# Routing six of the eight groups inside the second attention, in place of five

## The reference, cut to what matters

```python
x = x + _L0_xattn_ref(_layernorm(x), ctx_2048, ...)
x = x + _L0_ffn_ref(_layernorm(x), ...)
x = x + _L1_xattn_ref(_layernorm(x), ctx_2048, ...)   # ends in a layer norm of its own
x = x + _L1_ffn_ref(_layernorm(x), ...)
```

```python
shared = jnp.maximum(normed @ sw1 + sb1, 0.0) @ sw2 + sb2
scores, idx = jax.lax.top_k(probs, TOPK)              # TOPK = 2 of E = 8
w = scores / (jnp.sum(scores, axis=-1, keepdims=True) + 1e-06)
```

## Time and profile before

| | us |
|---|---|
| median of 3 runs | 1467.87 (1464.55 to 1470.46) |
| the profiled execution, its own time | 1472.39 |
| span in that profile | 1470.6 |
| `attention1`, its last instruction ends | 1161.86 |
| `sorted_experts`, its first instruction starts | 1163.17 |
| its first expert matmul starts | 1195.53 |

### The profile page before, as it was taken

How to read it: one execution, slowest core, us unless ns; L and a number is a source line. 1 busy time by engine, 2 the same in 40 slices (tenths; PEclk the granted TensorE clock), 3 DMA queues, 4 the chain that set the end, 5 groups by cost and what they waited for, 6 DMA issues and landing times. The chain is left out here.

```text
span 1470.6 us, 35946 instructions
## 1 busy us (share of the span) xinstructions
PE 1252.5 (85%) x13401; PEld 1044.1 (71%) x13401; DVE 1053.2 (72%) x2080; ACT 898.4 (61%) x1699; POOL 652.2 (44%) x677
## 2 busy tenths in 40 slices
PE   4999998399999999997699999999996268999780
PEld 3777776278777877785589888888885256788660
DVE  5888888566777687775356678989887477687563
ACT  3888887566565656554455655666654258788560
POOL 3222222145555565564332345556664435066461
PEclk9999999699999999999799999999999559999995
DMA  4222221332212221321300000000000122147536
GB/s 142 93 93 93 94 93 64 116 94 80 73 48 82 80 73 43 87 80 48 100 26 10 10 16 10 17 20 17 20 14 16 50 74 84 31 152 252 178 125 183
DMA packets 88373, 109.64 MB, mean 75 GB/s; under 512 B 13322, under 2 KB 55050, under 8 KB 88202
## 3 DMA queue, kind: packets, MB, share of 16 engines
q1 hardware_dynamic: 83210, 97.05, 21.1%
q0 software_dynamic: 4992, 10.30, 2.1%
HBM read 61.70 MB, written 29.82 MB: 62 GB/s over the span
## 5 line engine op out<-in xcount | busy, mean ns | idle before, releaser
L830 POOL TENSOR_TENSOR b_h_lo<-b_h,b_h_hi 128x512 fp32r<-128x512 f32 x168 | 216.5, 1294 | 179.3 <-ACT b_h_hi L854 178.9
L849 ACT ACTIVATE b_zg<-b_zg 128x512 f32<-128x512 f32 x168 | 97.6, 581 | 82.0 <-PE b_zg L894 81.8
L854 ACT ACTIVATE b_h_hi<-b_h 128x512 fp32r<-128x512 f32 x168 | 105.1, 626 | 65.4 <-DVE b_h L1059 65.3
L2173 POOL DMA_INDIRECT planes_dram<-d_y_out,d_back x92 | 94.0, 1022 | 106.7 <-DVE d_y_out L2484 83.6
L1059 DVE TENSOR_TENSOR b_h<-b_zg,b_uw 128x512 f32<-128x512 f32 x168 | 116.1, 691 | 32.0 <-ACT b_zg L849 26.7
L1052 DVE TENSOR_TENSOR b_uw<-b_zu,b_gw 128x512 f32<-128x512 f32 x128 | 88.1, 688 | 57.7 <-PE b_zu L894 50.9
L2453 DVE TENSOR_TENSOR d_h_lo<-d_h,d_h_hi 128x512 fp32r<-128x512 f32 x124 | 85.1, 690 | 48.4 <-ACT d_h_hi L2214 37.2
L312 POOL TENSOR_TENSOR a_qx<-a_qT,headmask 128x256 f32<-128x256 f32 x64 | 37.9, 613 | 149.3 <-ACT a_qT L347 149.3
L519 DVE TENSOR_REDUCE a_top<-a_score_ps 128x8 f32<-128x1024 f32 x64 | 78.0, 1218 | 18.6 <-PE a_score_ps L410 18.6
L1293 POOL TENSOR_TENSOR c_prob<-c_prob,c_recip 128x512 f32<-128x512 f32 x64 | 65.5, 1044 | 50.9 <-DVE c_recip L1709 50.9
L1716 DVE TENSOR_TENSOR c_oT_lo<-c_oy,c_oT_hi 128x512 fp32r<-128x512 f32 x64 | 43.7, 683 | 58.3 <-ACT c_oT_hi L1421 57.8
(11 more groups left out here) (393 smaller groups left out, 4175.2 us busy)
## 6 DMA issues: line engine op xcount, KB each, us to landing
rows_dram<-a_blank SPq DMA_DIRECT2D x32, 520.0 KB, 3.3
b_gw<-gates_dram SPq DMA_DIRECT2D x64, 256.0 KB, 3.8
d_up_slot<-d_up_tab SPq DMA_DIRECT2D x15, 512.0 KB
d_down_slot<-d_down_tab SPq DMA_DIRECT2D x15, 512.0 KB
d_xg<-rows_dram SPq DMA_DIRECT2D x23, 260.0 KB
b_gm<-gates_dram SPq DMA_DIRECT2D x32, 160.0 KB, 3.9
c_craw<-in_c_ctxT_dram SPq DMA_DIRECT2D x16, 256.0 KB, 3.0
d_pay<-planes_dram SPq DMA_DIRECT2D x12, 256.0 KB, 4.2
```

The lines of the kernel that those rows point to most:

```text
L830: pool.tensor_tensor(h_lo[:, m % HS, :], h[:, m % HF, :], h_hi[:, m % HS, :].bitcast(F32), ALU.subtract).then_inc(lo_done.sem, 1)
L849: act.activation(zg_ps[:, n % ZG, :], zg_ps[:, n % ZG, :], ACT.Silu).then_inc(sg_done.sem, 1)
L854: act.activation(h_hi[:, m % HS, :], h[:, m % HF, :], ACT.Copy).then_inc(hi_done.sem, 1)
L2173: pool.indirect_dma_start(planes, bass.IndirectOffsetOnAxis(ap=back[:, t, u:u + 1], axis=0), y_out[:, t % 2, u, :], None).then_inc(added[t ...
```

## The change

One constant. Group 5 (the sixth) is now routed in `attention1`, at ticks 30 to 38, and its eight scatters take the place of group 4's at the head of `sorted_experts`; group 4's eight scatters move into ticks 35, 36 and 37. `sorted_experts` routes two groups (6 and 7) in place of three.

```diff
@@ -36,7 +36,7 @@
 UNITS = B * N // P
 GROUP = 4
 GROUPS = UNITS // GROUP
-ROUTED = 5
+ROUTED = 6
 COLS = GROUP * P
 H = 16
 PAIRS = H // 2
```

## The result

The changed kernel takes **1483.01 us** (median of 5 runs, 1477.84 to 1486.4), the kernel before on the same chip 1468.63 (1464.55 to 1472.79). The ratio is **1.0075, 95% interval 1.0046 to 1.0103**: slower, by 0.75%. Forecast were 1475.7 us and +7.8 us; the medians differ by 14.4, and 1483.01 stands at the upper end of the range that was given (1468 to 1483).

A forecast was written before the change was run, and what follows sets the result against it. PE bounds the attention's middle, but in its drain no engine does, only a chain of short steps. Drain loss 13.9 less last-stage gain 6.1 gives +7.8 us; 1467.87 + 7.8 = 1475.7 us, range 1468 to 1483.

The forecast's parts named there:

- T: Time the attention's drain loses by routing group 5 there: 13.9 us, its last instruction ending at 1175.8 instead of 1161.9.
- The six scatters: POOL's queue behind the last compare: six scatters of group 4 take 7.4 us ahead of unit 31's output scaling.
- the two last ones: Group 4's last two scatters, on POOL behind unit 31's output scaling: 0.15 + 2.4 us, landing 1.40 later.
- DVE's own detour is hidden: Drain's end: DVE's choose(5), 2.05 us ahead of the normalisation, is hidden under POOL's scatters.
- The shift up to tick 34: Drain: group 5's added steps shift the chain by 0.8 + 0.35 = 1.2 us (rounded), lower bound 0.
- The drain's end: End of the attention, what the drain loses without the earlier shift: 12.7 us.
- The fill, 3.2 us behind the landing: Drain's end: group 5's fill waits for the last scatters' landing, takes 3.2 us and ends the attention at 1175.8.
- Table loads hidden: Drain, ACT: two more function set switches for group 5, 1.28 us per load, hidden under other work.
- S: Time the last stage gives back with one group less to route: 2.9 + 3.15 = 6.1 us, bounds 2.9 and 10.2.
- Gives back all of it: Rival, last stage: PE's clock stays high and POOL's pieces are no limit, S = 13.2, total 1468.6 us; chance 0.2.
- The drain hides the routing: Rival, drain: half-idle engines hide the routing, T only 1.2 us, total 1463.0 us; chance 0.07.
- One more stall: Rival, drain: a second unexplained ACT wait adds 3.5 us, total 1479.2, or 1482.4 with S at its lower bound; chance 0.15.

The follow-up runs named there:

- e1: The changed kernel with three of group 4's scatters put ahead of group 5's compare in POOL's queue; ratio to before 1.011.
- e2: The changed kernel with all eight of group 4's scatters behind the last output scaling; ratio to before 1.0208.
- f1: The changed kernel with group 4's payload in its own memory, its eight scatters at the last stage's head, DVE splitting all weight pieces; 1442.27 us, ratio 0.9966.
- e6: The changed kernel without group 5's router products (POOL multiplies 8 values in place of 1024, routing by stale products); 1476.77 us, ratio to before 1.0116.
- e3: The kernel before with DVE splitting all of the last stage's weight pieces, POOL none; ratio to before 1.0012.
- e4: The changed kernel with DVE splitting all of the last stage's weight pieces, POOL none; ratio to before 1.005.
- e5: The changed kernel with a second payload tile, so group 5's fill and place don't wait for group 4's scatters; ratio to before 1.011.
- f3: The changed kernel with only the first unit's two copies of group 5's fill made, the other six left out; ratio to before 1.0104.
- f2: The changed kernel with group 4's payload in its own memory and its eight scatters at the last stage's head, weight splits unchanged; 1453.27 us, ratio 1.0029.
- r0: The changed kernel run again, unedited, beside others on one chip; 1477.53 us, ratio to before 1.0121.

## Why the prediction was right and where not

The sign and the mechanism held, the size did not: +7.8 was forecast, the medians differ by 14.4. That the result still falls in the range is in part luck of direction: T was priced too low, and had it been as much too high, the change would hardly have been told from none.

- **The six scatters (7.4), the two last ones (2.55), landing 1.40**: measured 7.51 from the first's start to the scaling, 2.79, 1.40. Right, and e1, e2 and f1 show that they are the cause: without them the stage starts 9.1 us earlier. That "DVE's own detour is hidden" was right too, and is also why only 4.1 of the 7.5 come back in e2: the 4.15 left are DVE's.
- **The shift up to tick 34, "1.2 us, rounded": the mis-sized term. It measured 5.4.** 3.8 arises by subtract(31): 0.8 for the variance steps as forecast, 3.0 for DVE standing still behind group 5's products (e6). I priced the products on POOL's timeline alone. The row to read was in the profile of before: there two instructions took long, each under a product of an earlier group, and 0.19 and 0.17 where none ran:
```profile
1062.15 1.45 DVE L1803 TENSOR_TENSOR c_raw<-c_raw,c_r_rstd 128x32 f32<-128x32 f32 x1
1073.93 2.22 DVE L1682 TENSOR_SCALAR c_top<-c_top 128x16 f32<-128x16 f32 x1
```
In the middle, with PE the bound, this was hidden; in the drain it is paid. The other 1.6 of the 5.4 I can't pin on one step, since after has two "remote" waits ahead of the output copy and before has one. e3 and e4 are the fairer pair: they have before's and after's attention, ran on one chip, and each has one such wait in the drain, of 2.77 and 2.76. There the output copy stands 28.41 and 29.45 behind subtract(31), so the term measures 3.8 + 1.0 = 4.9. The 1.0 is fill(4), whose slack the forecast held to cover the delay ("If it were gone, up to 1.2 us would be paid"): in e4 fill(4) waits 4.41 us for group 3's last scatter and the copy follows it without a gap, and in e5, where fill(4) waits for none of group 3's, the copy stands at 28.22. (In after 0.70 us lie between the two, so there the fill does not hold the copy.)
- **The drain's end**, from the output copy to the stage's start: 22.66 in after and 10.12 in before, 12.5 us more, where the forecast had 12.7.
- **The fill, 3.2 us behind the landing**: right in sum, wrong in mechanism. Stage start behind last scatter's end was forecast as 1.4 + 3.2 + 1.3 (the gap of before), 5.9; it is 5.07. But with the fill shortened or moved it stays (f3, e5).
- **Table loads hidden**: right, with no drain behind them.
- **S = 6.1**: 6.7 in after, and by the mechanism named. e4, and f1 against f2, show the limit that I named, POOL's pieces.
- **The rivals.** "Gives back all of it" did not come true, but an S near its 13.2 did in e4 (13.0), with another edit, and there the clock rose too: 43 to 53 us behind the stage's start PE had 0.66 of its clock in before, 0.83 in after and 1.00 in e4. "The drain hides the routing" fell with the 18.0. "One more stall": a second "remote" wait did appear in after, but most of T's excess is the products' (3.0): e3 and e4, with one such wait each, still give T = 68.20 - 50.79 = 17.4.
- **What the profiles don't explain.** Their stages sum to +10.6 us and the medians differ by 14.4, because before's profiled execution (1472.39) was 3.8 us above its median and after's was its median. But r0 and f3 differ from their before by 15.6 and 14.6 as well, and f3 has no "remote" wait. T would be larger without such waits: f3 takes 67.76 from subtract(30) to the stage's start, and before without one would take about 48.2 (e3's 50.79 less the 2.6 by which the copy comes later in e5, with one wait, than in f1, with none). This estimate gives T = 19.6, and with S = 6.9 (98.29 - 91.37) +12.7; the last 2 us of f3's 14.6 stay open.

## What to carry to other kernels

In a drain, where each engine waits for the next, price an added instruction not only in its own queue but for every engine that runs beside it: look for rows of before where the neighbours' short instructions are long under the same operation. Work that needs nothing from the drain, like scatters issued into an in-order queue, belongs where that queue is idle (here the last stage's head, where the next routing comes 31 us behind the start), even at the price of a second buffer; it was worth 9 us behind the compare and 3 ahead of it. And before paying for an end to come earlier, ask what stands beside it: the last fill was covered by a wait of equal length, and DVE's splits showed no gain in the whole time of before and 10 us of the last stage in f1.

## What the hardware did that I had not expected

- DVE instructions of 16 and 32 values a partition took 2.16 and 1.44 us in place of 0.17 and 0.19 while POOL multiplied 128x1024, and ended 0.03 to 0.05 behind it.
- In the eight profiles in which group 4's scatters stand at the attention's end, the next stage started 5.06 to 5.39 us behind the last one's end on POOL, in f3 3.67 behind its landing. Without one near it started 0.73 behind DVE's last step (f1).
- Some of ACT's waits (and in after one of DVE's, 3.96 us) have no releaser but "remote". The waits of e4 and of before, over the whole span, and none in f1, f2 and f3:
```profile
ACT d_h L2208 <- remote: 20.5, 5, 6.7
ACT c_oT_hi L1421 <- remote: 2.8, 1, 2.8
```
```profile
ACT d_h L2208 <- remote: 10.3, 2, 5.6
ACT c_oT_hi L1421 <- remote: 3.5, 1, 3.5
```
They occur in all ten profiles from the other chips, 7 to 23 us in sum on ACT, always behind 1060 us, and on the third chip of the experiments in none of three. The stretch from the first routed tile to the final sums, in which no edit changed an instruction (f1 and f2 have its input buffer elsewhere), took 175 to 194 us with them and 168.5 to 170.4 without; there 15 runs of before lay within 3 us (1446.88 to 1449.8), on the chip of e3 22 within 15 (1458.95 to 1474.4). What they are was not tried. I take them for the reason why single times of this kernel tell little under 10 us; distances between marks tell more.
